# A Mamba kernel with experts: the skip term moves from TensorE to VectorE, the product with silu(z) from VectorE to GpSimd

## Chip, cores, metric

The kernel runs on one core of a Trainium2 chip. The metric is the device time of one execution in microseconds (us), lower being better. Several executions are timed and their median is taken. One further execution is recorded by the hardware profiler.

## What is computed

The input x has 4 sequences of 1024 tokens and 256 channels. It is normalised per token, and two branches use the result. One is eight Mamba layers in a row; the other is a top-1 mixture of eight experts. The output is x + s * silu(experts). The change touches the Mamba layers alone:

```
for i in range(8):
    x = x + mamba_layer(x, ...)
def mamba_layer(x, Wi, cw, cb, Wx, Wdt, bdt, Alog, Dp, Wo):
    xin, z = split(x @ Wi.T, 2)                    # 512 channels each
    u = silu(causal_conv(xin, cw, cb))             # 4 taps
    dt_raw, B, C = split(u @ Wx.T, [16, 16, 16])
    delta = softplus(dt_raw @ Wdt.T + bdt)
    for t in range(1024):                          # the scan, 16 states for each channel
        h = h * exp(delta[t] * A) + (delta[t] * u[t]) * B[t]
        y[t] = sum over states of h * C[t]
    y = (y + u * Dp) * silu(z)
    return y @ Wo.T
```

## The kernel before

The work of the layers is cut into 64 units: 8 layers, 4 sequences, 2 halves of 512 tokens. Even units are the first half of a sequence (`h == 0`), odd ones the second, whose scans start from the state that the first half left (`carry`). Channels lie on the 128 partitions in `CB` = 4 blocks, tokens along the free dimension.

Inside a unit U there are 64 steps: 16 states n times 4 blocks j, numbered k = 4n + j. Each engine walks through these steps (n, j) in its own program and does, at fixed places, the other work of the unit and the preparation of the next two. The places are tables written out by hand at the head of the file (`GATE_AT`, `CONV_AT`, `SOFT_AT`, `RING_AT` and so on). The engines keep in step by semaphores. For one step k:

- GpSimd multiplies `du` (delta times u) by the row of B into `drive` (L884). There are `DRIVE` = 8 drive tiles, so drive k waits until scan k - 8 is over (L883). SyncE fetches the rows of B (`brep`) ahead of it.
- ScalarE makes the decay, exp(delta * A), into one of two PSUM tiles `ps_d` (L916); the exponential k waits for scan k - 2.
- VectorE runs the recurrence over the 512 tokens (`scan`, L1077), which needs decay and drive.
- When the four blocks of a state are scanned, TensorE transposes the state tokens-first into a ring of two PSUM tiles (L1231), ScalarE multiplies by C as it leaves PSUM (`weigh`, L923), and TensorE transposes it back and adds it up in `ps_y` (L1238), whose banks the diagonal products opened.

At places between these, in the unit's order:

- `skip_y` (L1249, TensorE, at (1, 1) and (1, 3)): four products of `u` with a diagonal 128x128 matrix of D, which start the sum in `ps_y`. The matrices of a layer (256 KB) are loaded by SyncE once a layer (L749, L832 to L835), after the last use of those before.
- `gate` (L1177, VectorE, at (1, 1) and three times at (1, 2)): the previous unit's `ps_y` times `zs`, which is silu(z), into `gated`, the tile `relu` under another name.
- two mark operations (L1088, L1090) and the scan of `alive` (L1101) on VectorE at rows 2 and 3, convolution steps of later units (L1114 for a first tap, L1118 for the others), the final sum of the residual `add_x` (L1183), softplus (L1137 to L1147) and `du` (L1127).
- `halo` (L863, L865, GpSimd, at (3, 2)), which waits for the last convolution step of the next unit, `mask_x` (L855, GpSimd, at (5, 1)), and `keep_carry` (L870, GpSimd, once for each state of a first half).
- at (4, 2), ScalarE's block: exponential 20, a table load, silu of the next unit's convolution (`silu_u`, L951), silu of this unit's z (`silu_z`, L955) and a second table load (L1029).
- `x_proj` (L1297) and `out_proj` (L1318) on TensorE; the latter reads `gated`.

Of the kernel before, what the change touches and what calls it, by code (L numbers as in the profile page):

```python
# [73 lines left out]
DRIVE = 8  # L74
# [15 lines left out]
HALO_AT, XM_AT = (3, 2), (5, 1)  # L90
CONV_ITEMS = [f"C{j}" for j in PE_CONV]
CV = CB - len(PE_CONV)
# [563 lines left out]
def mamba(nc, w_in, w_x, w_dt, w_out, w_skip, w_conv, a_log, par, xres, ident, alive_dram, bc_dram, rate_dram):  # L656

    with ExitStack() as ctx:
# [10 lines left out]
        skip = sb("skip", [P, CB, P])  # L669
# [10 lines left out]
        u = sb("u", [P, CB, T])  # L680
# [23 lines left out]
        skip_in, skip_used, conv_w_in = sem("skip_in"), sem("skip_used"), sem("conv_w_in")  # L704
# [27 lines left out]
        def _(sp):  # L732
# [15 lines left out]
            def load_skip(layer):  # L748
                sp.dma_start(skip[:], w_skip[:, layer * CB:(layer + 1) * CB, :]).then_inc(skip_in, 16)  # L749

# [39 lines left out]
            load_skip(0)  # L790
# [11 lines left out]
            for U in range(UNITS):  # L802
                kind = "first" if U == 0 else "last" if U == UNITS - 1 else "near" if U == UNITS - 2 else "mid"
                layer = U // UPL
                if U and kind != "last":
                    load_cur(U + 1, (U + 1) // UPL)
                if kind in ("first", "mid"):
                    load_taps(U, kind, U + 2, (U + 2) // UPL)
                for n in range(BREP, 2 * BREP):
                    load_brep(U, n)  # L810
                if kind in ("first", "mid"):
                    store_alive(U, kind, U + 2)
                if U and U % UPL == 0:

                    sp.wait_ge(ring_ready, item_ready(U, kind, "O1"))
                    load_out(layer)
                for n in range(2 * BREP, STATES):
                    load_brep(U, n)
                if kind != "last":
                    store_bc(U, kind, U + 1)  # L820
                if kind != "last":
                    for n in range(BREP):
                        load_brep(U + 1, n)
                if U % UPL == UPL - 2 and layer + 1 < LAYERS:

                    sp.wait_ge(ring_ready, item_ready(U, kind, "DT3"))
                    load_x(layer + 1)
                    sp.wait_ge(ring_ready, item_ready(U, kind, "Z3"))
                    load_inz(layer + 1)
                    sp.wait_ge(ring_ready, item_ready(U, kind, CONV_ITEMS[-1]))  # L830
                    load_conv(layer + 1)
                if U % UPL == UPL - 1 and layer + 1 < LAYERS:  # L832

                    sp.wait_ge(skip_used, U + 1)
                    load_skip(layer + 1)  # L835
                if U % UPL == UPL - 3 and layer + 1 < LAYERS:

                    sp.wait_ge(ring_ready, item_ready(U, kind, "X3"))
                    load_inx(layer + 1)
# [4 lines left out]
        def _(pool):  # L844
# [57 lines left out]
            units(pool, unit)  # L902

        @block.scalar
        def _(act):
# [40 lines left out]
            def silu_u(U, kind, F):  # L946
                act.wait_ge(conv_done, CV * F + CV)
                act.wait_ge(ring_act, item_read(U, kind, CONV_ITEMS[-1]))
                if not is_first(F):
                    act.wait_ge(skip_used, F)  # L950
                nc.scalar.activation(u[:], xc[:], ACT.Silu).then_inc(u_set, 1)  # L951
# [65 lines left out]
            def unit(U, h, it, kind):  # L1017
                for n in range(STATES):
                    for t in range(TC):
                        k = CB * n + t + 2  # L1020
                        if k < TILES:
                            exponent(U, h, k)
                        elif kind != "last":
                            exponent(U + 1, 1 - h, k - TILES)
                        if (n, t) == SILU_AT:
                            if kind != "last":
                                silu_u(U, kind, U + 1)
# [17 lines left out]
            for n in range(STATES):  # L1045
                for t in range(TC):
                    if (n, t) == SILU_AT:
                        silu_u(0, "pre1", 0)
# [3 lines left out]
            exponent(0, 0, 0)  # L1052
            exponent(0, 0, 1)
# [5 lines left out]
        def _(dve):  # L1059
            def scan(U, h, it, kind, n, j):  # L1060
# [3 lines left out]
                if j == 0:  # L1064
# [10 lines left out]
                    if h == 1 and n < 3:  # L1075
# [45 lines left out]
            def make_du(F, hf, p):  # L1121
# [5 lines left out]
                nc.vector.tensor_tensor(du[:, pair, :], delta[hf][:, pair, :], u[:, pair, :], ALU.mult).then_inc(du_set, 1)  # L1127
# [57 lines left out]
            def unit(U, h, it, kind):  # L1185
                for n in range(STATES):
                    for j in range(CB):
                        scan(U, h, it, kind, n, j)
                        for i in range(CB):
                            if (n, j) == GATE_AT[i] and kind != "first":  # L1190
                                gate(U - 1, 1 - h, i)
# [19 lines left out]
            for j in range(CB):  # L1211
                gate(UNITS - 1, 1, j)
# [4 lines left out]
        def _(pe):  # L1217
# [74 lines left out]
            def x_proj(U, h, kind, F, it):  # L1292
# [3 lines left out]
                for k in range(CB):  # L1296
                    last = nc.tensor.matmul(out[0:XD, :], w_x_sb[:, k, :], u[:, k, :], start=(k == 0), stop=(k == CB - 1))  # L1297
# [31 lines left out]
            def late(U, h, hf, kind, F, it, n, t):  # L1329
# [4 lines left out]
                if (n, t) == RING_AT["XD"]:  # L1334
                    x_proj(U, h, kind, F, it)
# [8 lines left out]
            def unit(U, h, it, kind):  # L1344
                past = kind_before(U, kind)
                for n in range(STATES):
                    for t in range(TC):
# [7 lines left out]
                        for j in range(CB):  # L1355
                            if (n, t) == SKIPY_AT[j]:
                                skip_y(U, kind, it, j)
# [177 lines left out]
```

## Time and profile before

| | |
|---|---|
| time, median of 3 runs | 7741.25 us (7739.77 to 7742.37) |
| the profiled execution's own time | 7743.71 us |
| its span, first to last instruction | 7742.0 us |
| TensorE busy | 6941.3 us, 39999 matmuls |
| VectorE busy | 6668.0 us |
| ScalarE busy | 6422.9 us |
| GpSimd busy | 5929.2 us |
| mean granted TensorE clock | 0.987 of full speed |

Busy time is the union of an engine's instructions; instructions of one engine overlap a little, so durations in a list can add up to more than the busy time. A row of a list has start, duration, engine, line, operation, the tiles written and read, and in brackets the idle time before it with the instruction that ended it.

### The profile page before, as it was taken

How to read it: one execution, taken by the hardware profiler on the slowest of the kernel's cores; microseconds unless marked ns; L12 is line 12 of the kernel's file. 1: busy time of each engine (PE TensorE's matmuls, PEld its weight loads, DVE VectorE, ACT ScalarE, POOL GpSimd, SP SyncE). 2: the span in 40 equal slices, each digit the busy share in tenths (PEclk: the TensorE clock that was granted, in tenths of full speed). 3: DMA queues.
4: the chain of work that ended last, by engine and by line, in shares of the span. 5: the costliest groups of instructions: out<-in, count | busy, mean ns of one | idle time of the engine just before them, and what ended most of it. 6: DMA issues, size and time to landing. Idle time of an engine off the chain costs nothing. (4 is left out here: it accounts for less than half of the span.)

```text
span 7742.0 us, 143629 instructions
## 1 busy us (share of the span) xinstructions
PE 6941.3 (90%) x39999; PEld 4801.8 (62%) x39999; DVE 6668.0 (86%) x6510; ACT 6422.9 (83%) x10314; POOL 5929.2 (77%) x4917
## 2 busy tenths in 40 slices
PE   6979999999999999999999999999999999999997
PEld 4646666666666666666666666666666666666665
DVE  3259988988998899889889988988998898889888
ACT  1258888888888888888888888888888888888887
POOL 2148887888888888888888887888888788888875
PEclk9989999999999999999999999999999999999998
DMA  4111111111111111111111111111111111111112
GB/s 161 34 42 40 40 39 47 43 39 40 42 45 44 39 39 48 42 40 39 40 46 44 40 38 41 45 42 39 39 48 42 39 40 41 45 43 39 40 39 91
DMA packets 222613, 352.40 MB, mean 46 GB/s; under 512 B 43856, under 2 KB 78448, under 8 KB 221712
## 3 DMA queue, kind: packets, MB, share of 16 engines
q1 hardware_dynamic: 218048, 332.70, 14.6%
q0 software_dynamic: 3792, 10.38, 0.4%
q8 instruction: 365, 5.98, 0.3%
q14 instruction: 408, 3.34, 0.1%
HBM read 325.00 MB, written 17.98 MB: 44 GB/s over the span
## 5 line engine op out<-in xcount | busy, mean ns | idle before, releaser
L884 POOL TENSOR_TENSOR drive<-du,brep 128x512 f32<-128x512 f32 x4096 | 5505.9, 1374 | 708.3 <-DVE du L1127 385.6
L916 ACT ACTIVATE ps_d<-delta,cur 128x512 f32<-128x512 f32 x4096 | 2869.9, 701 | 373.9 <-DVE state L1077 354.8
L923 ACT ACTIVATE prod<-ps_r,cT 128x512 f32<-128x512 f32 x4096 | 2837.1, 693 | 245.4 <-PE ps_r L1231 243.9
L1231 PE MATMUL ps_r<-ident,state 128*128 128x128 f32 x16384 | 2564.0, 280 | 297.1 <-ACT prod L923 158.3
L1077 DVE TENSOR_TENSOR_SCAN state<-ps_d,carry,drive 128x512 f32<-128x512 f32 x2048 | 2517.7, 1266 | 260.6 <-ACT ps_d L916 258.5
L1077 DVE TENSOR_TENSOR_SCAN state<-ps_d,drive 128x512 f32<-128x512 f32 x2048 | 2396.8, 1206 | 245.6 <-ACT ps_d L916 233.0
L1238 PE MATMUL ps_y<-ident,prod 128*128 128x128 f32 x16384 | 2481.9, 276 | 25.9 <-ACT prod L923 25.9
L1238 PEld LDWEIGHTS ps_y<-ident,prod 128*128 128x128 f32 x16384 | 1938.9, 142 | 666.8 <-issue 499.4
L1231 PEld LDWEIGHTS ps_r<-ident,state 128*128 128x128 f32 x16384 | 1851.3, 142 | 729.9 <-ACT prod L923 462.5
L1278 PE MATMUL ps_r<-xm,w_inz_sb 128*128 128x512 f32 x1024 | 507.4, 618 | 81.6 <-ACT prod L923 81.6
L1270 PE MATMUL ps_r<-xm,w_inx_sb 128*128 128x512 f32 x1024 | 509.1, 620 | 21.9 <-ACT prod L923 14.2
L1318 PE MATMUL ps_r<-relu,w_out_sb 128*128 128x512 f32 x1024 | 473.9, 606 | 58.6 <-ACT prod L923 56.0
L1118 DVE SCALAR_TENSOR_TENSOR xc<-xpad,taps,xc 128x512 f32<-128x512 f32 x576 | 506.6, 880 | 2.6
L870 POOL COPY carry<-state 128x4 f32<-128x4 f32 x512 | 227.2, 444 | 222.2 <-DVE state L1077 222.1
L1311 PE MATMUL ps_r<-xdbl,w_dt_sb 16*128 16x512 f32 x512 | 295.0, 656 | 86.7 <-DVE xres L1183 52.1
L1318 PEld LDWEIGHTS ps_r<-relu,w_out_sb 128*128 128x128 f32 x1024 | 184.7, 190 | 272.8 <-issue 217.4
L1278 PEld LDWEIGHTS ps_r<-xm,w_inz_sb 128*128 128x128 f32 x1024 | 173.6, 189 | 260.4 <-ACT prod L923 126.7
L1270 PEld LDWEIGHTS ps_r<-xm,w_inx_sb 128*128 128x128 f32 x1024 | 175.1, 190 | 193.1 <-issue 149.3
L535 ACT ACTIVATE hid<-ps_t,b_sb 128x128 f32<-128x128 f32 x312 | 85.0, 383 | 227.4 <-PE ps_t L496 227.3
L1114 DVE TENSOR_SCALAR xc<-xpad,taps 128x512 f32<-128x512 f32 x192 | 189.2, 985 | 93.2 <-ACT xpad L929 93.2
L463 POOL DMA_INDIRECT ys_dram<-yb,row x39 | 37.5, 962 | 296.9 <-DVE yb L555 296.9
L1297 PE MATMUL ps_r<-u,w_x_sb 128*48 128x512 f32 x512 | 234.1, 601 | 33.3 <-ACT u L951 33.3
(144 smaller groups left out, 4647.3 us busy)
## 6 DMA issues: line engine op xcount, KB each, us to landing
brep<-bc_dram SPq DMA_DIRECT2D x1024, 256.0 KB, 3.2
w_sb<-w SPq DMA_DIRECT2D x8, 1024.0 KB
w_all<-w SPq DMA_DIRECT2D x8, 1024.0 KB, 11.4
xb<-xs_dram SPq DMA_DIRECT2D x39, 128.5 KB, 2.0
w_all<-x SPq DMA_DIRECT2D x4, 1024.0 KB, 9.1
w_inx_sb<-w_in SPq DMA_DIRECT2D x8, 512.0 KB, 4.1
w_inz_sb<-w_in SPq DMA_DIRECT2D x8, 512.0 KB, 4.5
w_out_sb<-w_out SPq DMA_DIRECT2D x8, 512.0 KB, 4.2
```

What stands on the lines that cost most here:

```text
L884: nc.gpsimd.tensor_tensor(drive[:, k % DRIVE, :], du[:, j, :], brep[:, n % BREP, :], ALU.mult).then_inc(drive_set, 1)
L916: nc.scalar.activation(ps_d[:, k % 2, :], delta[h][:, j, :], ACT.Exp, scale=cur[h][:, a:a + 1]).then_inc(decay_set, 1)
L923: nc.scalar.activation(prod[:, t, :], ps_r[:, item_place(U, h, kind, item), :], ACT.Copy, scale=cT[(h + 1) % 2 if item[1] == "prev" else h ...
L1077: nc.vector.tensor_tensor_scan(state[STATE_IN[n]][:, j, :], ps_d[:, k % 2, :], drive[:, k % DRIVE, :], carry[:, n, j:j + 1] if h == 1 else ...
L1118: step = nc.vector.scalar_tensor_tensor(xc[:, j, :], xpad[:, j, tap:tap + T], w, xc[:, j, :], ALU.mult, ALU.add)
L1231: last = nc.tensor.transpose(out[:, j * P:(j + 1) * P], state[STATE_IN[n]][:, j, t * P:(t + 1) * P], ident[:])
L1238: last = nc.tensor.matmul(ps_y[:, j, t * P:(t + 1) * P], prod[:, t, j * P:(j + 1) * P], ident[:], start=False, stop=True, is_transpose=Tru ...
L1270: last = nc.tensor.matmul(out, w_inx_sb[:, k, j * P:(j + 1) * P], xm[h][:, k, :], start=(k == 0), stop=(k == DB - 1))
L1278: last = nc.tensor.matmul(out, w_inz_sb[:, k, j * P:(j + 1) * P], xm[hf][:, k, :], start=(k == 0), stop=(k == DB - 1))
L1297: last = nc.tensor.matmul(out[0:XD, :], w_x_sb[:, k, :], u[:, k, :], start=(k == 0), stop=(k == CB - 1))
L1311: nc.tensor.matmul(out, w_dt_sb[:, j * P:(j + 1) * P], xdbl[0:RANK, :], start=True, stop=True).then_inc(ring_ready, 1)
L1318: last = nc.tensor.matmul(out, w_out_sb[:, j, k * P:(k + 1) * P], gated[:, j, :], start=(j == 0), stop=(j == CB - 1))
```

## The change

The sum in `ps_y` now starts with the first state's transposed-back tile (`start=(item[1] == 0)` in `turn_back`), which waits until the previous unit's `ps_y` has been read. The diagonal products, their matrices and their loads go; `skip` becomes a tile of D itself, 32 columns, loaded once. Where VectorE multiplied by `zs`, it now computes u * D + `ps_y` into `gated`, at the same places. GpSimd multiplies `gated` by `zs` in place, one block at each of the steps (3, 0) to (3, 3), behind that step's drive, and `out_proj` and the copy of the next z wait for that. Since `u` is read later than before, there are two u tiles in turn; to hold them, the drive tiles go from 8 to 4, so drive k waits for scan k - 4. The list of exponentials is written as a table (`DECAYS`) with two empty lists of exceptions, and the condition of one carry wait is put in another form (`last < 0` for `n < 3`).

```
-DRIVE = 8
+DRIVE = 4
+BOOST_AT, REST_AT = [], []
-GATE_AT, SKIPY_AT = [(1, 1), (1, 2), (1, 2), (1, 2)], [(1, 1), (1, 3), (1, 3), (1, 3)]
+GATE_AT, ZED_AT = [(1, 1), (1, 2), (1, 2), (1, 2)], [(3, 0), (3, 1), (3, 2), (3, 3)]
...
-        u = sb("u", [P, CB, T])
+        u = [sb(f"u{h}", [P, CB, T]) for h in range(2)]
...
-                if U % UPL == UPL - 1 and layer + 1 < LAYERS:
-
-                    sp.wait_ge(skip_used, U + 1)
-                    load_skip(layer + 1)
...
+            def gate(U, h, j):
+
+                if j == 0:
+                    pool.wait_ge(z_set, U + 1)
+                wait_counted(gated_done, CB * U + j + 1)
+                nc.gpsimd.tensor_tensor(gated[:, j, :], gated[:, j, :], zs[h][:, j, :], ALU.mult).then_inc(zed, 1)
...
+                        for i in range(CB):
+                            if (n, j) == ZED_AT[i] and kind != "first":
+                                gate(U - 1, 1 - h, i)
...
+            for j in range(CB):
+                gate(UNITS - 1, 1, j)
...
-                    act.wait_ge(gated_done, CB * (F - 1))
+                    act.wait_ge(zed, CB * (F - 1))
...
-            def gate(U, h, j):
+            def add_skip(U, h, it, j):
 
                 if j == 0:
                     dve.wait_ge(back_done, TILES * U + TILES)
-                    dve.wait_ge(z_set, U + 1)
-                nc.vector.tensor_tensor(gated[:, j, :], ps_y[:, j, :], zs[h][:, j, :], ALU.mult).then_inc(gated_done, 1)
+                    dve.wait_ge(skip_in, 16)
+                nc.vector.scalar_tensor_tensor(gated[:, j, :], u[h][:, j, :], skip[:, bass.ds((it // BATCH) * CB + j, 1)], ps_y[:, j, :],
+                                               ALU.mult, ALU.add).then_inc(gated_done, 1)
...
+                if item[1] == 0 and t == 0 and kind != "first":
+                    pe.wait_ge(gated_done, CB * U)
                 for j in range(CB):
                     last = nc.tensor.matmul(ps_y[:, j, t * P:(t + 1) * P], prod[:, t, j * P:(j + 1) * P], ident[:],
-                                            start=False, stop=True, is_transpose=True, skip_group_check=True)
+                                            start=(item[1] == 0), stop=True, is_transpose=True, skip_group_check=True)
...
-            def skip_y(U, kind, it, j):
-
-                if kind != "first":
-                    pe.wait_ge(gated_done, CB * (U - 1) + j + 1)
-                if j == 0:
-                    pe.wait_ge(skip_in, 16 * (it // BATCH) + 16)
-                    pe.wait_ge(u_set, U + 1)
-                last = nc.tensor.matmul(ps_y[:, j, :], skip[:, j, :], u[:, j, :], start=True, stop=True, skip_group_check=True)
-                if j == CB - 1:
-                    last.then_inc(skip_used, 1)
...
-                pe.wait_ge(gated_done, CB * V + CB)
+                pe.wait_ge(zed, CB * V + CB)
```

## Rows read from the trace of the kernel before

**Rows 1.** The page, busy time, share and instructions of each engine.

```profile
PE 6941.3 (90%) x39999; PEld 4801.8 (62%) x39999; DVE 6668.0 (86%) x6510; ACT 6422.9 (83%) x10314; POOL 5929.2 (77%) x4917
```

**Rows 2.** The instructions of L951 and of L1114: duration min/median/max, first and last start.

```profile
L951 ACT ACT_TABLE_LOAD  x64: 1283/1283/1283, 469.2 to 7510.8; - x64
...
L1114 DVE TENSOR_SCALAR xc<-xpad,taps x192: 514/547/2268, 459.1 to 7478.6; 128x512 f32<-128x512 f32 x192
```

**Rows 3.** Timeline of VectorE in an odd unit: start, duration, instructions, idle before.

```profile
3993.80 1.13 DVE L1118 SCALAR_TENSOR_TENSOR xc<-xpad,taps,xc 128x512 f32<-128x512 f32 x1
...
4001.46 2.45 DVE L1077 TENSOR_TENSOR_SCAN state<-ps_d,carry,drive 128x512 f32<-128x512 f32 x2
4003.83 0.66 DVE L1088 TENSOR_SCALAR low<-xres 128x1024 bf16 x1
...
4008.56 0.72 DVE L1118 SCALAR_TENSOR_TENSOR xc<-xpad,taps,xc 128x512 f32<-128x512 f32 x1
...
4011.57 7.13 DVE L1077 TENSOR_TENSOR_SCAN state<-ps_d,carry,drive 128x512 f32<-128x512 f32 x6
...
4025.95 1.28 DVE L1077 TENSOR_TENSOR_SCAN state<-ps_d,carry,drive 128x512 f32<-128x512 f32 x1 [3.56 <-ACT ps_d L916]
...
4095.26 2.35 DVE L1127 TENSOR_TENSOR du<-delta,u 128x1024 f32<-128x1024 f32 x2
```

**Rows 4.** Timeline of ScalarE in the same unit.

```profile
4012.86 0.69 ACT L916 ACTIVATE ps_d<-delta,cur 128x512 f32<-128x512 f32 x1 [1.05 <-DVE state L1077]
...
4017.61 0.69 ACT L916 ACTIVATE ps_d<-delta,cur 128x512 f32<-128x512 f32 x1
...
4034.10 0.69 ACT L916 ACTIVATE ps_d<-delta,cur 128x512 f32<-128x512 f32 x1 [2.17 <-DVE state L1077]
```

**Rows 5.** Timeline of GpSimd in the same unit.

```profile
3993.12 9.54 POOL L884 TENSOR_TENSOR drive<-du,brep 128x512 f32<-128x512 f32 x7
4009.61 0.20 POOL L863 COPY xpad<-xpad 128x12 f32<-128x12 f32 x1 [6.95 <-DVE xc L1118]
4009.76 8.66 POOL L884 TENSOR_TENSOR drive<-du,brep 128x512 f32<-128x512 f32 x7
...
4096.64 7.39 POOL L884 TENSOR_TENSOR drive<-du,brep 128x512 f32<-128x512 f32 x5 [6.72 <-DVE du L1127]
```

**Rows 6.** Groups by line and shape: count, busy us, mean ns, idle before.

```profile
L1118 DVE SCALAR_TENSOR_TENSOR xc<-xpad,taps,xc 128x512 f32<-128x512 f32 x576 | 506.6, 880 | 2.6
...
L1249 PE MATMUL ps_y<-u,skip 128*128 128x512 f32 x512 | 241.0, 593 | 0.1
...
L1114 DVE TENSOR_SCALAR xc<-xpad,taps 128x512 f32<-128x512 f32 x192 | 189.2, 985 | 93.2 <-ACT xpad L929 93.2
...
L1177 DVE TENSOR_TENSOR relu<-ps_y,zs 128x512 f32<-128x512 f32 x256 | 160.9, 667 | 5.1 <-PE ps_y L1238 5.1
```

**Rows 7.** Timeline of TensorE in the odd unit.

```profile
3998.99 1.02 PE L1249 MATMUL ps_y<-u,skip 128*128 128x512 f32 x2
...
4000.73 2.74 PE L1249 MATMUL ps_y<-u,skip 128*128 128x512 f32 x6
...
4016.59 3.70 PE L1318 MATMUL ps_r<-relu,w_out_sb 128*128 128x512 f32 x8 [0.53 <-ACT prod L923]
```

**Rows 8.** Timeline of VectorE: the even unit before, and L1114 in both.

```profile
3882.42 1.08 DVE L1118 SCALAR_TENSOR_TENSOR xc<-xpad,taps,xc 128x512 f32<-128x512 f32 x1
...
3890.16 2.33 DVE L1077 TENSOR_TENSOR_SCAN state<-ps_d,drive 128x512 f32<-128x512 f32 x2
...
3899.86 6.77 DVE L1077 TENSOR_TENSOR_SCAN state<-ps_d,drive 128x512 f32<-128x512 f32 x6
...
3918.43 1.15 DVE L1114 TENSOR_SCALAR xc<-xpad,taps 128x512 f32<-128x512 f32 x1 [1.33 <-ACT xpad L929]
...
4029.98 2.10 DVE L1114 TENSOR_SCALAR xc<-xpad,taps 128x512 f32<-128x512 f32 x1 [1.05 <-ACT xpad L929]
```

**Rows 9.** Timeline of GpSimd: a drive of the even unit.

```profile
3882.90 1.73 POOL L884 TENSOR_TENSOR drive<-du,brep 128x512 f32<-128x512 f32 x1
```

More of the change, by code:

```diff
@@ L90 @@
 HALO_AT, XM_AT = (3, 2), (5, 1)
+LEAD = 2
 CONV_ITEMS = [f"C{j}" for j in PE_CONV]
+DECAYS, at = {}, LEAD
+for n, j in [(n, j) for n in range(STATES) for j in range(CB)]:
+    count = 1 + BOOST_AT.count((n, j)) - REST_AT.count((n, j))
+    DECAYS[n, j] = list(range(at, at + count))
+    at += count
 CV = CB - len(PE_CONV)
@@ L668, in mamba @@
         taps = [sb(f"taps{h}", [P, NTAP]) for h in range(2)]
-        skip = sb("skip", [P, CB, P])
+        skip = sb("skip", [P, LAYERS * CB])
         minus_ones = sb("minus_ones", [P, P], BF16)
@@ L789, in _ @@
             load_inz(0)
-            load_skip(0)
+            sp.dma_start(skip[:], w_skip).then_inc(skip_in, 16)
             load_out(0)
@@ L944, in copy_c, with silu_u @@
                                      bias=taps[hf][:, COL_CB + j:COL_CB + j + 1]).then_inc(ring_act, 1)
-            def silu_u(U, kind, F):
+            def silu_u(U, kind, F, hf):
                 act.wait_ge(conv_done, CV * F + CV)
                 act.wait_ge(ring_act, item_read(U, kind, CONV_ITEMS[-1]))
-                if not is_first(F):
-                    act.wait_ge(skip_used, F)
-                nc.scalar.activation(u[:], xc[:], ACT.Silu).then_inc(u_set, 1)
+                if kind == "mid" or kind == "near":
+                    act.wait_ge(gated_done, CB * (F - 1))
+                nc.scalar.activation(u[hf][:], xc[:], ACT.Silu).then_inc(u_set, 1)
             def silu_z(U, h, kind):
@@ L1019, in unit @@
                     for t in range(TC):
[L1020 to L1024, printed above, removed]
+                        for k in DECAYS[n, t]:
+                            if k < TILES:
+                                exponent(U, h, k)
+                            elif kind != "last":
+                                exponent(U + 1, 1 - h, k - TILES)
                         if (n, t) == SILU_AT:
                             if kind != "last":
-                                silu_u(U, kind, U + 1)
+                                silu_u(U, kind, U + 1, 1 - h)
                             silu_z(U, h, kind)
@@ L1047, in _ @@
                     if (n, t) == SILU_AT:
-                        silu_u(0, "pre1", 0)
+                        silu_u(0, "pre1", 0, 0)
                         nc.scalar.preload_act_table_set(TABLE)
@@ L1051, in _ @@
                     early(0, 0, "pre1", 1, n, t)
-            exponent(0, 0, 0)
-            exponent(0, 0, 1)
+            for k in range(LEAD):
+                exponent(0, 0, k)
             units(act, unit)
@@ L1074, in scan @@
                         dve.wait_ge(carried, STATES * it + last + 1)
-                    if h == 1 and n < 3:
+                    if h == 1 and last < 0:
                         dve.wait_ge(carried, STATES * it + last + STATES + 1)
@@ L1126, in make_du @@
                     dve.wait_ge(drive_set, TILES * F - 2 + 2 * p)
-                nc.vector.tensor_tensor(du[:, pair, :], delta[hf][:, pair, :], u[:, pair, :], ALU.mult).then_inc(du_set, 1)
+                nc.vector.tensor_tensor(du[:, pair, :], delta[hf][:, pair, :], u[hf][:, pair, :], ALU.mult).then_inc(du_set, 1)
             def softplus(F, hf, p, part):
@@ L1190, in unit @@
                             if (n, j) == GATE_AT[i] and kind != "first":
-                                gate(U - 1, 1 - h, i)
+                                add_skip(U - 1, 1 - h, it - 1 + h, i)
                         if (n, j) in ADD_AT and kind != "first":
@@ L1211, in _ @@
             for j in range(CB):
-                gate(UNITS - 1, 1, j)
+                add_skip(UNITS - 1, 1, ITERS - 1, j)
             for k in range(DB):
@@ L1290, in conv_pe, with x_proj @@
                 last.then_inc(ring_ready, 1)
-            def x_proj(U, h, kind, F, it):
+            def x_proj(U, h, hf, kind, F, it):
                 out = place(U, h, kind, "XD")
@@ L1296, in x_proj @@
                 for k in range(CB):
-                    last = nc.tensor.matmul(out[0:XD, :], w_x_sb[:, k, :], u[:, k, :], start=(k == 0), stop=(k == CB - 1))
+                    last = nc.tensor.matmul(out[0:XD, :], w_x_sb[:, k, :], u[hf][:, k, :], start=(k == 0), stop=(k == CB - 1))
                 last.then_inc(ring_ready, 1)
@@ L1334, in late @@
                 if (n, t) == RING_AT["XD"]:
-                    x_proj(U, h, kind, F, it)
+                    x_proj(U, h, hf, kind, F, it)
                 if (n, t) == RING_AT["BC"]:
@@ L1354, in unit @@
                             turn_state(U, h, kind, ("S", n - 1, t), U, n - 1, t)
-                        for j in range(CB):
-                            if (n, t) == SKIPY_AT[j]:
-                                skip_y(U, kind, it, j)
                         for k in range(DB):
@@ L1512 @@
         "w_out": blocks(a["attn_W_out"].transpose(0, 2, 1), CB),
-        "w_skip": diagonals(a["attn_D_par"]),
+        "w_skip": by_layer("D_par"),
         "w_conv": diagonals(taps),
```

4 lines of the change are left out of this document (1 added, 3 removed).

## The prediction

> **What bounds the kernel now.** The page's busy shares come first: TensorE 90%, VectorE 86%, ScalarE 83%, GpSimd 77% [rows 1]. No engine is alone at its limit, so a share can't say what one saved or added operation is worth; the place in the period of one unit must. 64 units of 512 tokens pass, one every 111.8 us on average: the 64 starts of silu(u) run from 469.2 to 7510.8 [rows 2]. Odd units (second half of a sequence) and even ones differ a little, so I read one of each.
>
> The timeline of VectorE in an odd unit [rows 3] shows a stretch with no idle mark, from the convolution step at 3993.80 (just before scan 5) to scan 19 at 4018.7. In it lie the four gates, two mark operations, two more convolution steps and the scan of alive. ScalarE comes next [rows 4]. The exponential at 4017.61 is that of scan 20; it waits for the end of scan 18 (the fifth of the six scans that begin at 4011.57 and take 7.13: it ends at 4017.5). Right behind it stand a table load, silu(u), silu(z) and a second load, and only then the exponential of scan 21; VectorE idled 3.56 us for it and began the scan at 4025.95 [rows 3]. So the unit goes: VectorE solid up to scan 18, then ScalarE's block, then the scans again. Whatever delays scan 18 delays the rest of the unit, and what TensorE does meanwhile is inside that cover unless it is very late.
>
> GpSimd [rows 5] runs up to eight tiles ahead. It finishes drive 14 early, waits 6.95 us for the last convolution step (halo, L863), then makes seven drives in 8.66 us, 1.24 each. It is ahead of VectorE throughout.
>
> **The change, part by part** (us per unit; "slower" positive).
>
> TensorE's diagonal products. Two passes of four products start 0.43 apart: 8 x 0.43 = 3.4 us per unit, and the group sums to 241 us over the run [rows 6, 7]. They stand at 3998.99 and 4000.73 to 4003.5, wholly inside VectorE's solid stretch, and ScalarE waited again for VectorE at 4012.86 (1.05 us), after they were done [rows 4]. I take 0. If that cover were gone it would be worth up to -3.4.
>
> The add of the skip term. VectorE's gate is a two-input operation with one input in PSUM, 667 ns [rows 6]. The new one adds a pointer scalar whose address is computed per unit. The nearest row is the convolution step, the same instruction with two SBUF inputs: 0.72 alone (4008.56) and 0.88 as a mean [rows 3, 6]. So 0 to 0.21 each; I take 0.06, as one input stays in PSUM: 4 x 0.06 = +0.25, range 0 to 0.8. All of it is before scan 18, so it counts in full.
>
> Products with silu(z) on GpSimd. Four 128x512 operations like a drive, 1.24 apart: 4 x 1.24 = 5.0 us of GpSimd. On average there is room (77% busy), but they are put between drives 12 and 16, and with four drive tiles drive k can't start before scan k-4 has ended. Odd unit: scan 8 is the first of the two scans from 4001.46 that take 2.45 together, and ends at 4002.7 [rows 3]. From there GpSimd must make drives 12 to 16 and the four products, nine operations: 9 x 1.24 = 11.15, plus the halo copy 0.15: 4014.0. Scan 16 started at 4011.57 + 2 x 1.175 = 4013.9. Late by 0.1 with GpSimd undisturbed. Even unit: scan 8 ends at 3891.35, 11.15 plus a carry copy (0.15) and the memset of the halo (0.05) gives 3902.7; scan 16 started at 3899.86 + 2 x 1.115 = 3902.1 [rows 8]. Late by 0.6.
>
> But GpSimd won't be undisturbed. Before, it stood idle from 4002.6 to 4009.6 [rows 5], while VectorE did two marks and a convolution step (0.66, 0.66, 0.72). The pairs [rows 5, 9] show that these engines hinder each other. A drive that meets a convolution step takes 1.73 in place of 1.24, and that step took 1.08 and 1.13 in place of 0.72 [rows 3, 8, 9]; the first convolution step (L1114) took 1.15 and 2.10 when drives ran beside it [rows 8]; its shortest is 0.51, its median 0.55 [rows 2]. With three such meetings at 0.45 each, GpSimd is later by 1.35; if VectorE gives way instead, it loses 0.3 to 1.5 a meeting, which is the same delay in another row. Scan 16 is then late by 1.45 (odd) and 1.95 (even); up to scan 18 GpSimd's pitch (1.24) against the scans' (1.175 and 1.115), and in even units another carry copy, add 0.1 and 0.4. Mean: (1.55 + 2.35)/2 = +2.0. Bounds: (0.2 + 1.0)/2 = 0.6 without any hindrance, 3.3 if each meeting costs 0.9.
>
> The Trainium skill, SBUF — State Buffer, section "SBUF: two separate sides", says that VectorE and GpSimd take a shared port pair as an exclusive lock for a whole instruction, and the loser blocks fully. By that, all 2.04 us of the three VectorE operations would be added to GpSimd's run in place of 1.35, and this term would be 2.7, which makes 7873 in all. The lengthened rows agree with its kind; no run here yet shows its size in this stretch.
>
> Fewer drive tiles, elsewhere. Later in the unit GpSimd has room again: xm and the drives after it have 6.5 us, the scans stand still during ScalarE's block. There the shorter lead helps. L1114 at 4029.98 (2.10 long) ran while GpSimd made drives 29 and 30, tiles that with four buffers can't be begun before scans 25 and 26. GpSimd will have done drive 26 by about 1.3 after scan 22 and then be silent, so L1114 takes some 0.6 (odd, gain 1.5) and 0.55 in place of 1.15 (even, gain 0.6). ScalarE waited 2.17 for the scan behind it [rows 4], so the gain is on the path: -1.05. Two more convolution steps in even units lie as well, worth some -0.3 to -0.4 in the mean. Sum -1.4, bounds 0 and -2.9: the whole excess of both convolution lines over their shortest times, 506.6 - 576 x 0.72 = 92 and 189.2 - 192 x 0.514 = 91 [rows 2, 6], over 63 units; 0.72 is the lone step of rows 3.
>
> The end of a unit. GpSimd used to be silent for 6.72 us until du was made [rows 5], and the last delta operations and both du (2.35 together) ran undisturbed [rows 3]. Now drives 62 and 63 fall there. Four operations can each be caught, by up to a drive's length; most start together with a scan's end, ahead of GpSimd. +0.5, bounds 0 and 1.4.
>
> At nothing: the second u buffer (its wait is for gates long past), the wait of the projections for the products (done near 4013.5; O0 started at 4016.59 [rows 7]), the turn-back's wait for the add of the skip term (it comes before scan 7, and the turn-back is TensorE's next row of work), the loads of skip that go from SyncE's queue (seven of 256 KB, behind which brep loads stood; each was hidden), the rewritten carry wait, and the list of exponentials, which stays in order. If the products were late for O0 they would cost what they are late beyond 3 us. The tail: the last four products run after the last adds, 4 x 1.24 against 0.6 a gate: +3 once.
>
> **Sum.** 0.25 + 2.0 - 1.4 + 0.5 = +1.35 per unit, x 63 = +85, and 3 at the end: 88. The profiled execution spans 7742.0 and lasted 7743.7, 2.5 above the median of three (7741.25), which is a third of a thousandth, so: 7741 + 88 = about 7829, or +1.1%.
>
> **Rivals.**
> 1. Faster, by relief of the contention. One mechanism: with a lead of four tiles GpSimd moves in step with the scans, and VectorE's two-input operations start ahead of it all through the unit. For it: the 183 us of excess; against: the crowded stretch between drives 12 and 16, of which the pairs above tell. It decides once that relief exceeds the lateness at scan 16. Relief 2.4 against 0.6 + 0.25 + 0.1: -1.45 x 63 = -91, so 7653 with the tail. Chance 0.14.
> 2. A cancelling of the two: lateness 1.3, relief 1.4, the rest 0.1. 7741 to 7752; chance 0.1.
> 3. TensorE's relief pays after all, -3.4 x 63 = -215 and the other terms as in the sum: 7614. Against it is VectorE's solid stretch. Chance 0.05.
> 4. The lock at full size, or VectorE losing at each meeting (2.10 in place of 0.52 shows that this happens): lateness 3.3, relief 1.0, du 1.2, adds 0.4: +3.9 x 63 = +246, 7990 at the worst, 7870 to 7920 more likely. Chance 0.18. For it: the rows of contended pairs; against: most pairs that start together cost one engine only. The rule cited above is the mild form of it.
>
> My forecast has 0.53. Within 0.2% (15 us, about what a measurement can tell from no change): the second rival's part, 0.1; faster 0.19; slower 0.71. Range 7700 to 7920; the forecast's own is 7765 to 7880.
>
> **What the next profile would show.** VectorE's solid stretch should break before scan 16, with GpSimd (L884) as the releaser, or else the marks (L1088, L1090) should be longer than 0.66. ScalarE's block should start 1.5 to 3 us later after scan 0. L1114 should fall from 985 ns to about 600. TensorE's share falls by 3 points. The gate line should show 0.67 to 0.75. I am wrong if GpSimd is never a releaser of a scan and the marks keep their 0.66, or if the removal of the diagonal products alone shortens the unit.

## The result

The changed kernel takes 7968.2 us (median of 4 runs, 7967.9 to 7970.5) where the kernel before took 7741.8: a ratio of 1.0293, 95% interval 1.0276 to 1.0311, 226 us slower. I had forecast 7829, with a range up to 7920. The direction was right, the size less than half of what came, and the time lies outside the range.

The page of the changed kernel, busy time and share, against [rows 1]:

```profile
PE 6841.5 (86%) x39487; PEld 4705.4 (59%) x39487; DVE 6728.4 (84%) x6510; ACT 6442.7 (81%) x10314; POOL 6442.9 (81%) x5173
```

TensorE lost 100 us of busy time, not the 241 of its diagonal products: `out_proj` alone got 66 us slower, and most of the rest is that instructions overlap less. VectorE gained 60, GpSimd 514. The groups by line show where; two groups of the kernel before come first, and [rows 6] have those that answer to L1130, L1126 and L1189 (there L1118, L1114 and L1177):

```profile
L1318 PE MATMUL ps_r<-relu,w_out_sb 128*128 128x512 f32 x1024 | 473.9, 606 | 58.6 <-ACT prod L923 56.0 <-DVE relu L1177 2.7
L1127 DVE TENSOR_TENSOR du<-delta,u 128x1024 f32<-128x1024 f32 x128 | 150.4, 1215 | 0.0
```

```profile
L1322 PE MATMUL ps_r<-relu,w_out_sb 128*128 128x512 f32 x1024 | 539.7, 676 | 139.2 <-ACT prod L935 133.1
...
L1130 DVE SCALAR_TENSOR_TENSOR xc<-xpad,taps,xc 128x512 f32<-128x512 f32 x576 | 482.4, 838 | 2.6
...
L1126 DVE TENSOR_SCALAR xc<-xpad,taps 128x512 f32<-128x512 f32 x192 | 107.1, 558 | 92.8 <-ACT xpad L941 92.8
L1189 DVE SCALAR_TENSOR_TENSOR relu<-u,skip,ps_y 128x512 f32<-128x512 f32 x256 | 176.0, 726 | 5.1 <-PE ps_y L1253 5.1
...
L1139 DVE TENSOR_TENSOR du<-delta,u 128x1024 f32<-128x1024 f32 x128 | 218.3, 1744 | 0.0
```

The adds of the skip term (L1189) take 0.73 where the gates took 0.67. L1126, the first convolution step, fell from 985 ns to 558: the relief that was forecast came. But `out_proj` (L1322) went from 606 to 676 ns a matmul, and du (L1139) from 1.21 to 1.74 us.

The timeline of VectorE in an even unit of the changed kernel, which begins at 3979.51; then GpSimd's in the same stretch:

```profile
3995.30 0.87 DVE L1100 TENSOR_SCALAR low<-xres 128x1024 bf16 x1
...
3997.22 0.66 DVE L1102 TENSOR_SCALAR low<-xres 128x1024 bf16 x1
...
4000.05 0.86 DVE L1130 SCALAR_TENSOR_TENSOR xc<-xpad,taps,xc 128x512 f32<-128x512 f32 x1
...
4004.65 1.22 DVE L1089 TENSOR_TENSOR_SCAN state<-ps_d,drive 128x512 f32<-128x512 f32 x1 [0.37 <-POOL drive L891]
4007.28 4.86 DVE L1089 TENSOR_TENSOR_SCAN state<-ps_d,drive 128x512 f32<-128x512 f32 x4 [1.41 <-POOL drive L891]
4015.64 0.69 DVE L1196 TENSOR_TENSOR xres<-xres,ps_r 128x512 f32 x1 [3.50 <-PE ps_r L1322]
...
4022.54 1.22 DVE L1089 TENSOR_TENSOR_SCAN state<-ps_d,drive 128x512 f32<-128x512 f32 x1 [2.04 <-ACT ps_d L928]
```

```profile
3995.58 1.72 POOL L877 TENSOR_TENSOR relu<-relu,zs 128x512 f32<-128x512 f32 x1
3997.26 1.75 POOL L891 TENSOR_TENSOR drive<-du,brep 128x512 f32<-128x512 f32 x1
3998.95 0.19 POOL L870 COPY carry<-state 128x4 f32<-128x4 f32 x1
3999.10 1.27 POOL L877 TENSOR_TENSOR relu<-relu,zs 128x512 f32<-128x512 f32 x1
4000.33 1.72 POOL L891 TENSOR_TENSOR drive<-du,brep 128x512 f32<-128x512 f32 x1
```

The solid stretch of VectorE breaks at scans 15 and 16, released by GpSimd's drives, and in GpSimd's own rows the marks and the convolution step have each lengthened an operation from 1.27 to 1.72 or 1.75: three meetings, as counted in the forecast. What was not in it stands one row later: VectorE waits 3.50 us for O0, the first eight matmuls of `out_proj`. O0 of an even unit of the kernel before, then TensorE's timeline in the changed kernel:

```profile
3905.06 3.67 PE L1318 MATMUL ps_r<-relu,w_out_sb 128*128 128x512 f32 x8 [0.78 <-ACT prod L923]
```

```profile
4007.26 0.66 PE L1244 MATMUL ps_r<-ident,state 128*128 128x128 f32 x4 [0.17 <-ACT prod L935]
4010.13 5.29 PE L1322 MATMUL ps_r<-relu,w_out_sb 128*128 128x512 f32 x8 [2.22 <-ACT prod L935]
```

The windows ahead of O0 and over it, first of the kernel before, then of the changed one (busy us and instructions of TensorE, its weight loads, VectorE, ScalarE and GpSimd; granted TensorE clock, DMA share, GB/s):

```profile
3900.00:3905.00 5.00, 3.71 (x28) 3.00 (x28) 5.00 (x5) 4.08 (x8) 5.00 (x6) 1.00 0.23 53
3905.00:3908.80 3.80, 3.74 (x11) 1.80 (x12) 1.63 (x2) 3.77 (x5) 3.80 (x4) 1.00 0.29 69
```

```profile
4003.00:4010.10 7.10, 3.71 (x28) 3.00 (x28) 5.25 (x6) 4.53 (x8) 7.10 (x9) 0.99 0.14 37
4010.10:4015.40 5.30, 5.27 (x10) 2.37 (x11) 2.03 (x2) 5.27 (x6) 5.30 (x5) 0.69 0.19 49
```

The same 28 matmuls that took TensorE 3.71 of 5.00 us before are spread over 7.10 us by the late scans, and then the granted clock of the next 5.3 us was 0.69, a mixture of the 2.4 and the 1.2 GHz level. The eight matmuls of O0 took 5.29 us, against 3.67. This is the rule in even units and not in odd ones: O0 took 5.16 us or more in all of the 29 even units from 4 to 60 and in 7 of the 30 odd ones from 3 to 61, and 3.67 to 3.70 in the same units before.

To see how much each place costs, I took from the traces the start of scan k after the unit's scan 0, averaged over 29 even and 29 odd units (3 to 60), and subtracted that of the kernel before (us, even / odd; k = 64 is the next unit's scan 0). Each column includes what lies to its left. The experiments, which follow below, stand in the same table.

| kernel | 12 | 18 | 22 | 31 | 58 | 60 | 64 |
|---|---|---|---|---|---|---|---|
| changed | 0.28/0.40 | 2.56/2.16 | 3.91/2.51 | 3.49/0.33 | 3.08/0.33 | 5.11/1.83 | 5.10/1.84 |
| 4 drive tiles alone | 0.20/0.26 | 0.19/0.26 | 0.19/0.26 | -0.24/-1.93 | -0.64/-1.92 | 1.38/-0.42 | 1.41/-0.41 |
| products of 8 columns | 0.51/0.58 | 0.65/0.65 | 0.65/0.65 | 0.22/-1.53 | -0.18/-1.53 | 1.84/-0.04 | 1.84/-0.02 |
| products early | 0.87/0.60 | 1.86/1.52 | 1.86/1.52 | 1.43/-0.66 | 1.02/-0.67 | 3.05/0.83 | 3.05/0.85 |
| du late | 0.39/0.61 | 2.66/2.37 | 3.84/2.34 | 3.42/0.16 | 3.01/0.16 | 2.49/-0.80 | 5.92/2.66 |
| transposes twice | 0.40/0.58 | 2.69/2.35 | 2.42/2.33 | 2.00/0.14 | 1.59/0.14 | 3.62/1.64 | 3.61/1.65 |
| no diagonals | -0.02/-0.01 | -0.04/0.07 | -0.04/0.06 | -0.05/-0.29 | -0.12/-0.29 | -0.12/-0.29 | -0.12/-0.25 |
| 4 tiles, du spread | 0.01/0.16 | 0.00/0.16 | -0.01/0.16 | -0.43/-2.02 | 1.00/-0.54 | -0.27/-1.95 | 0.80/-0.81 |
| products in row 2, du spread | 1.44/1.14 | 2.43/2.06 | 2.42/2.06 | 1.98/-0.14 | 3.39/1.31 | 2.13/-0.10 | 3.19/1.04 |
| lead of 4 at 60 to 63 | -0.07/0.00 | -0.06/0.00 | -0.06/0.00 | -0.08/-0.19 | -0.10/-0.21 | 1.42/1.07 | 1.41/2.13 |
| lead of 4 at 20 to 31 | 0.02/0.00 | 0.02/-0.01 | 0.02/0.00 | -0.41/-2.19 | 0.77/0.02 | 0.77/0.01 | 0.77/0.05 |
| lead of 4 at 20 to 39 | -0.05/0.00 | -0.04/-0.01 | -0.04/0.00 | -0.48/-2.19 | -0.59/-0.62 | 0.31/-0.48 | 0.30/0.14 |
| lead of 4 at 24 to 28 | 0.00/0.00 | 0.00/-0.01 | 0.01/0.00 | -0.42/-2.18 | -0.35/-0.34 | -0.35/-0.34 | -0.35/-0.35 |

In the changed kernel a unit is 3.47 us longer in the mean, and 63 of them make 219 of the 226 us. Three places pay: up to scan 18 (2.36), steps 18 to 22 of even units (1.35 there), and the du stretch between scans 58 and 60 (2.03 and 1.50).

### The profile page after: what moved, and what is told of

Its sections match the earlier page's. It is cut to its first block and busy times, and to the rows that moved or that the text cites. A ratio compares the mean times of both kernels' runs of the same rounds, so it can differ in the third digit from the quotient of the medians.

```text
span 7968.7 us, 143200 instructions
## 1 busy us (share of the span) xinstructions
PE 6841.5 (86%) x39487; PEld 4705.4 (59%) x39487; DVE 6728.4 (84%) x6510; ACT 6442.7 (81%) x10314; POOL 6442.9 (81%) x5173
## 5 line engine op out<-in xcount | busy, mean ns | idle before, releaser
L891 POOL TENSOR_TENSOR drive<-du,brep 128x512 f32<-128x512 f32 x4096 | 5741.2, 1422 | 1070.7 <-DVE state L1089 946.4
L1244 PEld LDWEIGHTS ps_r<-ident,state 128*128 128x128 f32 x16384 | 1822.6, 141 | 1076.4 <-ACT prod L935 782.9
L1322 PE MATMUL ps_r<-relu,w_out_sb 128*128 128x512 f32 x1024 | 539.7, 676 | 139.2 <-ACT prod L935 133.1
L1130 DVE SCALAR_TENSOR_TENSOR xc<-xpad,taps,xc 128x512 f32<-128x512 f32 x576 | 482.4, 838 | 2.6
L1322 PEld LDWEIGHTS ps_r<-relu,w_out_sb 128*128 128x128 f32 x1024 | 208.1, 213 | 395.9 <-issue 360.7
L877 POOL TENSOR_TENSOR relu<-relu,zs 128x512 f32<-128x512 f32 x256 | 352.6, 1378 | 8.2 <-issue 8.2
L1196 DVE TENSOR_TENSOR xres<-xres,ps_r 128x512 f32 (+1 forms) x128 | 88.1, 688 | 208.3 <-PE ps_r L1322 208.3
```

The source lines that it names most:

```text
L877: nc.gpsimd.tensor_tensor(gated[:, j, :], gated[:, j, :], zs[h][:, j, :], ALU.mult).then_inc(zed, 1)
L891: nc.gpsimd.tensor_tensor(drive[:, k % DRIVE, :], du[:, j, :], brep[:, n % BREP, :], ALU.mult).then_inc(drive_set, 1)
L1130: step = nc.vector.scalar_tensor_tensor(xc[:, j, :], xpad[:, j, tap:tap + T], w, xc[:, j, :], ALU.mult, ALU.add)
L1244: last = nc.tensor.transpose(out[:, j * P:(j + 1) * P], state[STATE_IN[n]][:, j, t * P:(t + 1) * P], ident[:])
L1322: last = nc.tensor.matmul(out, w_out_sb[:, j, k * P:(k + 1) * P], gated[:, j, :], start=(j == 0), stop=(j == CB - 1))
```

## The experiments

Ratios are against the kernel before on the same chip, with their 95% interval. The chips differ a little: the kernel before had a median of 7739.2 to 7744.8 us beside the experiments, so a difference of two experiments' times can be off by up to 6 us.

**Four drive tiles alone.**

```
-DRIVE = 8
+DRIVE = 4
```

> The kernel before with 4 drive tiles in place of 8 and nothing else. Theory A (the loss of the change is made in three places: GpSimd's crowded run between drives 12 and 16, TensorE's halved clock behind it, and drives 62 and 63 that now lie in front of du): only the third place is left, about +1.1 us per unit, against a gain of 1.5 in odd and 0.6 in even units from L1114; together 7740 to 7790 us. Theory B (the shorter lead itself costs, all over the unit): most of the 226 us, so above 7880.

7779.0 us, ratio 1.0052 (1.0035 to 1.0068), inside theory A's range: the shorter lead costs almost nothing up to scan 22, gains up to scan 31 (0.43 and 2.19) and loses 2.02 and 1.50 between scans 58 and 60. Both sizes were underestimated, a loss of 1.76 per unit in the mean for the 1.1 expected and a gain of 1.3 by scan 31 for 1.05, and the total is right since they offset each other. Of the 226 us the shorter lead explains about 38. The du stretch of an odd unit, VectorE and then GpSimd:

```profile
4106.20 1.62 DVE L1144 TENSOR_TENSOR low<-low,delta 128x1024 f32<-128x1024 f32 x1
4107.73 1.27 DVE L1077 TENSOR_TENSOR_SCAN state<-ps_d,carry,drive 128x512 f32<-128x512 f32 x1
4108.93 1.19 DVE L1147 TENSOR_TENSOR delta<-low,relu 128x1024 f32<-128x1024 f32 x1
4110.05 3.42 DVE L1127 TENSOR_TENSOR du<-delta,u 128x1024 f32<-128x1024 f32 x2
```

```profile
4104.22 7.03 POOL L884 TENSOR_TENSOR drive<-du,brep 128x512 f32<-128x512 f32 x4
4114.74 2.68 POOL L884 TENSOR_TENSOR drive<-du,brep 128x512 f32<-128x512 f32 x2 [3.49 <-DVE state L1077]
```

The two du took 2.35 before [rows 3] and 3.42 here. The last of the four drives (number 63) ends at 4111.25; it was free to start when scan 59 was over, had to let L1147 end, and then, by these rows, went ahead of the first du. L1144 took 1.62 in place of 1.20, since drive 61 was already running when it began. By the traces' means L1144 costs 0.83 in even and 0.42 in odd units, the two du 1.07 and 1.08: nearly the whole of the 2.02 and 1.50. In the code the second du also waits for drive 63, since it overwrites what that reads.

**Products of 8 columns.** GpSimd multiplies 8 of the 512 columns by silu(z); the others are left unmultiplied, which changes what is computed.

```
-nc.gpsimd.tensor_tensor(gated[:, j, :], gated[:, j, :], zs[h][:, j, :], ALU.mult)
+nc.gpsimd.tensor_tensor(gated[:, j, 0:8], gated[:, j, 0:8], zs[h][:, j, 0:8], ALU.mult)
```

> The changed kernel, but GpSimd multiplies only 8 of the 512 columns of each block by silu(z); the other columns are left unmultiplied, so the output is not the reference's. Theory A: the run of GpSimd between drives 12 and 16 loses its four times 1.24 us, scan 18 starts at most 0.4 later than in the kernel before, TensorE has no pause and keeps its clock; 7750 to 7800 us. Theory B (the lead): still above 7880. Theory C (the add of the skip term with its computed address costs more than the 0.25 us per unit of the sum): above 7850 too, with the lengthened operations in the profile.

7806.0 us, ratio 1.0087 (1.0071 to 1.0104), 6 us above theory A's range, with scan 18 later than the 0.4 that it allowed. Without the length of the products 162 us of the 226 are gone, scan 18 is 0.65 late in place of 2.36, and O0 takes 3.70 in every unit: the clock's part of the loss goes with the late scans. The rest, 27 us above 4 tiles alone, bounds what the adds of the skip term and the four small operations cost, less whatever TensorE's relief gives.

**Products early.**

```
-ZED_AT = [(3, 0), (3, 1), (3, 2), (3, 3)]
+ZED_AT = [(2, 1), (2, 2), (2, 2), (2, 3)]
```

> The changed kernel with the four products of GpSimd at steps (2,1), (2,2), (2,2), (2,3), where its trace shows GpSimd idle while VectorE adds the skip terms, in place of (3,0) to (3,3). Theory A: the same 5 us of GpSimd's work cost nothing there, scan 18 is late by 0.3 to 0.8, TensorE's clock stays at 2.4 GHz before O0; 7750 to 7820 us. Rival (GpSimd's work delays the scans wherever it stands, through the shared port): 7900 or more.

7873.5 us, ratio 1.0171 (1.0154 to 1.0188): 95 us better than the changed kernel and 50 to 120 worse than I expected, between the ranges of theory A and of the rival. The products cost something there too: the run is 67 us above the one with 8 columns. Scan 13 waited behind a convolution step that had itself to wait for GpSimd (1.62 in place of 0.72):

```profile
4070.62 2.68 DVE L1089 TENSOR_TENSOR_SCAN state<-ps_d,carry,drive 128x512 f32<-128x512 f32 x2
4073.22 1.62 DVE L1130 SCALAR_TENSOR_TENSOR xc<-xpad,taps,xc 128x512 f32<-128x512 f32 x1
4074.76 1.27 DVE L1089 TENSOR_TENSOR_SCAN state<-ps_d,carry,drive 128x512 f32<-128x512 f32 x1
```

What it saves is more than the scans' lateness: in even units scans 18 and 22 are late by the same 1.86, so O0 no longer adds anything.

**Du late.**

```
-DU_AT = [(14, 3), (14, 3)]
+DU_AT = [(15, 0), (15, 1)]
```

> The changed kernel with the two du operations at steps (15,0) and (15,1) in place of both at (14,3). Theory A: drives 62 and 63 no longer stand in front of the second du, VectorE loses less there: 0.6 to 1.2 us per unit, 7890 to 7930 us. Rival (the first drives of the next unit come too late now, as they wait for du): equal to the changed kernel or slower, with GpSimd as the releaser of scans 0 to 3.

8016.4 us, ratio 1.0355 (1.0338 to 1.0373), 48 us slower than the changed kernel. That is the rival's outcome, but not its mechanism: no scan from 0 to 3 of the next unit waits for GpSimd. Scan 60 starts 2.6 us earlier than in the changed kernel, as the two du now stand behind it, and scan 62 is 0.8 later: in the unit that I looked at, the second du takes 1.41 in place of 1.21 and the convolution step behind it 1.50 in place of 0.52, beside drives 64 and 65. The meeting was moved, not avoided.

**No diagonals.** The kernel before without the four diagonal products; u * D is missing in what is computed.

```
-                last = nc.tensor.matmul(ps_y[:, j, :], skip[:, j, :], u[:, j, :], start=True, stop=True, skip_group_check=True)
                 if j == CB - 1:
-                    last.then_inc(skip_used, 1)
+                    pe.sem_inc(skip_used, 1)
...
-                                            start=False, stop=True, is_transpose=True, skip_group_check=True)
+                                            start=(item[1] == 0), stop=True, is_transpose=True, skip_group_check=True)
```

> The kernel before without the four diagonal products of a unit: the sum in ps_y starts with the first transposed-back tile, the term u * D is left out of the output, all else stays (8 drive tiles, gates on VectorE, loads of skip). Theory A (TensorE's 3.4 us per unit lie in the cover of VectorE's solid stretch): within 10 us of 7740; the start of scan 18 after scan 0 moves by less than 0.1 us. Rival (TensorE's share of 90% was a bound): down to 7530. Second rival (the idle time lowers TensorE's clock later in the unit): 10 to 60 us slower, with more stretches at half the granted clock than the 24 of before.

7728.8 us, ratio 0.9977 (0.9966 to 0.9987). Scan 18 didn't move (-0.04, 0.07), as theory A had it, but the time lies just outside its 10 us: 16 us are gained, mostly in odd units behind scan 22, of the 215 that TensorE's 3.4 us per unit would have been. Where exactly they come from is open. O0 keeps its 3.67 to 3.70 and there are 24 stretches at half the granted clock, as many as before, so taking the products away doesn't by itself lower the clock at O0.

**Transposes twice.** To keep TensorE busy while the scans are late.

```
+TWICE_AT = [(2, 1), (2, 2), (2, 3), (3, 0), (3, 1)]
...
-                for j in range(CB):
-                    last = nc.tensor.transpose(out[:, j * P:(j + 1) * P], state[STATE_IN[n]][:, j, t * P:(t + 1) * P], ident[:])
+                for r in range(2 if (n, t) in TWICE_AT else 1):
+                    for j in range(CB):
+                        last = nc.tensor.transpose(out[:, j * P:(j + 1) * P], state[STATE_IN[n]][:, j, t * P:(t + 1) * P], ident[:])
```

> The changed kernel with the transposes of five state tiles (state 2 from its second token block on, and two of state 3) made twice over the same place, so that TensorE is busier by 0.44 us each in the stretch in which it now waits for the late scans. Theory A (O0 takes 5.29 us in place of 3.67 in even units since TensorE's clock fell to half, and scans 20 and 22 are late for that): O0 is back near 3.7, scan 22 of even units is 1.5 earlier, 7890 to 7930 us. Rival (what is late there is GpSimd's product or ScalarE's order, and the clock only goes with it): 7968 or, with the added work on the path, up to 8000.

7919.6 us, ratio 1.0222 (1.0205 to 1.0239), inside theory A's range: more work on TensorE and 49 us less time. Its windows and its O0 in an even unit that begins at 3955.46:

```profile
3979.00:3986.00 7.00, 5.35 (x46) 4.77 (x44) 5.13 (x6) 4.60 (x8) 7.00 (x9) 1.00 0.10 38
3986.00:3991.40 5.40, 5.00 (x17) 2.54 (x18) 3.49 (x4) 5.37 (x6) 5.40 (x5) 1.00 0.15 52
```

```profile
3986.09 3.70 PE L1324 MATMUL ps_r<-relu,w_out_sb 128*128 128x512 f32 x8 [1.73 <-ACT prod L936]
```

Busy for 5.35 of 7.00 us, TensorE keeps the full clock and O0 takes 3.70 again, in 63 of the 64 units. Scan 22 of even units is late by 2.42 in place of 3.91, while scan 18 is as late as before. Even units are 1.49 shorter and odd ones 0.19, together 52 us for 31 pairs, against the measured 49 (52 if each run is taken against the kernel before on its own chip). So this part of the loss is the clock, not GpSimd's product, and it is a consequence of the late scans.

**Four tiles, du spread.**

```
-SOFT_AT = [(7, 3), (8, 3), (9, 3), (10, 2), (10, 3), (11, 3), (14, 2), (14, 3)]
+SOFT_AT = [(7, 3), (8, 3), (9, 3), (10, 2), (10, 3), (11, 3), (14, 1), (14, 2)]
-DU_AT = [(14, 3), (14, 3)]
+DU_AT = [(14, 3), (15, 0)]
```

> The kernel before with 4 drive tiles, the last two softplus operations at (14,1) and (14,2) in place of (14,2) and (14,3), and the two du at (14,3) and (15,0). Theory A (of what 4 tiles alone cost, 1.5 to 2.0 us per unit come from the first du waiting behind drive 63, and the rest of the unit gains 0.6 to 1.9): the first du no longer meets drive 63, 7660 to 7720 us, faster than the kernel before. Rival (the crowding only moves): equal to the 7779 of the run with 4 tiles alone.

7744.2 us, ratio 0.9998 (0.9989 to 1.0008): 35 us better than 4 tiles alone and equal to the kernel before, not the 20 to 80 faster that I expected. The two du are no longer lengthened, which saves 1.0 to 1.1 us per unit, but scan 60 now waits 0.8 us until its state tile is free, which the two du had covered.

**Products in row 2, du spread.** The changed kernel with the placing above and

```
+ZED_AT = [(2, 0), (2, 1), (2, 2), (2, 3)]
```

> The changed kernel with GpSimd's four products at (2,0) to (2,3) and the same placing of softplus and du as in the run above. Theory A: against the run with the products at (2,1) to (2,3) (7873) one product fewer stands before drive 13, 0.5 to 1 us per unit, and du gives back 1 to 1.8: 7730 to 7790 us. Rival (GpSimd is short of time wherever the products stand): 7850 or more.

7884.1 us, ratio 1.0176 (1.0159 to 1.0193). The rival was right. From scan 31 to the unit's end the new placing of du gives back some 0.4 us per unit (1.21 and 1.18 lost there, 1.62 and 1.51 with the products early), but one product earlier doesn't help: scan 8 is already 1.0 late (the convolution step before it took 1.41 in odd and 1.68 in even units), scan 18 2.43 and 2.06 in place of 1.86 and 1.52. I tried three placings of the products, and none brought the design under 7873.

**A lead of four at some steps only.** These keep 8 tiles and change one wait of GpSimd in the kernel before; the range stood at `k >= 60`, `20 <= k < 32`, `20 <= k < 40` and `24 <= k < 29`.

```
-pool.wait_ge(scanned, TILES * U + k + 1 - DRIVE)
+pool.wait_ge(scanned, TILES * U + k + 1 - (4 if k >= 60 else DRIVE))
```

> The kernel before with its 8 drive tiles, but drives 60 to 63 of a unit wait for the scan four steps back. Theory A (the cost of 4 tiles is made at du, by drives 62 and 63 that fall among the last softplus operations and du): +1.5 to +2.0 us per unit, 7835 to 7870 us. Rival (the loss of 4 tiles at du is one of the whole lead, not of these drives): within 20 us of 7742.

7854.8 us, ratio 1.0142 (1.0127 to 1.0158). Four drives held back at the end of a unit cost 110 us, and the rival is refuted. Between scans 58 and 60 it is 1.52 and 1.28, of the 2.02 and 1.50 with 4 tiles at all steps; in odd units another 1.06 comes behind, since L1114 at step 61 takes 1.58 in place of 0.52.

> The kernel before with its 8 drive tiles, but drives 20 to 31 of a unit wait for the scan four steps back in place of eight; the other drives run ahead as before. Theory A (what 4 tiles gain is the first convolution steps behind ScalarE's block that no longer stand behind two drives, and what they lose is made at du): the gain without the loss, -0.4 us in even and -1.9 in odd units by step 31, as in the run with 4 tiles alone, about 7660 to 7690 us. Rival (the gain of that stretch is given back at the next wait, or the caught-up drives disturb VectorE later by as much): 7720 to 7745.

7765.6 us, ratio 1.0026 (1.0017 to 1.0035). The gain comes to the hundredth as with 4 tiles alone (-0.41 and -2.19 at scan 31) and is given back before scan 39, where GpSimd catches up: L1137, a softplus operation at step 31, takes 1.62 and 1.70 in place of 0.75 and 0.67. The rival had the mechanism; the time is 20 us above its range as well.

> The same for drives 20 to 39. Theory A: as above, and L1114 at step 38 of even units gains another 0.6; 7640 to 7680 us, if GpSimd still gets ahead of VectorE before du. Rival (GpSimd can't get ahead any more in the 20 drives that are left, and meets the last softplus operations): between the run above and 7780.

7757.5 us, ratio 1.0018 (1.0008 to 1.0027). Neither range was hit: 78 us above theory A, 8 below the rival's. It is the same give-back, later: even units still have -0.59 at scan 58 and lose 0.90 by scan 60, at du.

> The kernel before with its 8 drive tiles; only drives 24 to 28 of a unit wait for the scan four steps back. Theory A (the relief of L1114 at step 22 is real and the runs with longer windows gave it back because GpSimd caught up while VectorE did the first softplus operations): GpSimd now catches up in steps 25 to 31, where VectorE has pauses of about 1 us; -0.4 us in even and about -1.2 in odd units remain, 7680 to 7710 us, faster than both kernels. Rival (catching up costs VectorE as much wherever it is done): 7735 to 7765.

7723.8 us, ratio 0.9978 (0.9969 to 0.9987), 18 us faster than the kernel before and the fastest kernel here with the whole computation. It lies between the two ranges, 14 us above theory A's: -0.35 in both kinds of unit, since odd ones give back 1.8 of their 2.18 between scans 31 and 39 (L1137 at step 31 takes 1.76 in place of 0.67). The step at stake, with the two drives gone from beside it (2.10 before, [rows 8]):

```profile
4020.01 0.59 DVE L1114 TENSOR_SCALAR xc<-xpad,taps 128x512 f32<-128x512 f32 x1 [1.05 <-ACT xpad L929]
```

## Why the prediction was wrong

Step by step, forecast against measured, us per unit (mean of even and odd):

- Diagonal products at nothing: measured -0.19 (no diagonals), 12 to 16 us in all. Nearly right: the cover holds up to scan 22, but the forecast had named any shortening by the removal alone as a sign of being wrong, and the ratio's interval excludes 1.
- The add of the skip term +0.25: 726 against 667 ns on the lines, 0.06 x 4 = 0.24. Right; the computed address added nothing that the lines show.
- The products of GpSimd, scan 18 late by 2.0, with the adds 2.25: measured 2.56 and 2.16, mean 2.36. Right in the mean, by the mechanism that was named: nine operations between scan 8's end and drive 16, three of them lengthened by 0.45. Even units were forecast at 2.60, odd ones at 1.80. The split is less exact than the sum: with products of 8 columns 0.65 of the lateness stays, so their length is worth 1.7 and not 2.0, and 0.2 is the shorter lead before scan 12, to which the forecast gave nothing. The Trainium skill, SBUF — State Buffer, section "Who interferes with whom", says that a VectorE instruction with two SBUF inputs, or in a mode that uses both ports, contends with a GpSimd instruction that reads SBUF, while one with at most one SBUF input outside those modes doesn't. The trace agrees: L1189, whose second tensor is in PSUM, took 0.71 to 0.75 in all its 256 instructions, many of them beside running drives.
- Fewer tiles elsewhere -1.4: measured in 4 tiles alone from scan 18 to 58 as -0.83 and -2.18, mean -1.5. Right in the mean, and partly by luck: the terms of the forecast gave even units about 1.3 and odd ones 1.5. L1114 at step 22 shrank as forecast, by 1.49 in odd and 0.60 in even units.
- The end of a unit +0.5, bound 1.4: measured 2.03 and 1.50, mean 1.77 in the changed kernel, and the same in 4 tiles alone. **This step failed.** I took it that most operations of VectorE which start with a scan's end go ahead of GpSimd. That holds for L1147, but L1144 finds a drive already running (+0.84 and +0.42), and drive 63 gets in between L1147 and the first du (+1.08). I also overlooked in the code that the second du must wait for drive 63 in any case. The run with only drives 60 to 63 held back shows that these drives cause 1.40 of the 1.77; the rest goes with the whole lead of four.
- "At nothing" for the wait of the projections, and "what TensorE does meanwhile is inside that cover": **this step failed too**. O0 didn't wait for the products, as forecast, but TensorE, idle beside the late scans, lost its clock, and O0 took 1.6 us longer: +1.35 in even and +0.35 in odd units by scan 22. The forecast listed no term for the clock, though its own late scans were going to leave TensorE idle just ahead of O0. The experiment that only adds transposes gives it 49 us.

The sum of the forecast was 1.35 per unit and 3.47 came. Of the difference of 2.12, du is 1.27; the clock is (1.49 + 0.19)/2 = 0.84; the other terms, +0.1 up to scan 18 and -0.1 for the tiles elsewhere, cancel. The range ended too low, at 7920, since the du term's bound was too low and no term stood for the clock; the rival that gave a larger loss had the right side, but for a reason that didn't occur (VectorE losing at every meeting between drives 12 and 16).

Settled by experiments: the cost of the products' length, of drives 60 to 63, of the clock, and that TensorE's relief was worth 16 us at most in the kernel before. Only argued from rows: that it is drive 63, and not 62, which the first du waits for. Not tried: the changed kernel with eight drive tiles, for which there is no room beside two u tiles.

## What to carry to other kernels

When work goes from the fullest engine to another, look first for the stretch where it stands: here TensorE's 90% was worth 0.2%, and 5 us per unit on an engine that was idle for 23% of the time cost 162 us, because they stood where that engine had a deadline. A buffer's depth is not only protection against waiting: it also sets which operations of the other engine the producer runs beside, and the same convolution step took 2.10 or 0.59 us by that. Relief in one place can be lost at the next: of three kernels that held the drives back only where this helps, one kept a gain. And an engine whose clock depends on its activity can punish a wait a second time, in the work that follows it.

## What the runs showed of the hardware

- A VectorE operation can lose to two GpSimd operations in a row (L1114: 2.10 us where 0.51 is its shortest) and gets its time back when these are moved away (0.59).
- Doubling 20 transposes a unit, 2.2 us more work for TensorE, made the kernel 49 us faster, as the granted clock stayed at 1.00 where it had been 0.69. Nothing but transposes was added.
- TensorE's granted clock fell more often in the changed kernel: 52 stretches at half the full rate, 181 us together, against 24 and 109 us before, counted in the clock records between 520 and 7660 us. The count alone says little: products of 8 columns had 54 stretches (188 us) and transposes twice 46 (157 us), yet O0 took 3.70 in all 64 units of the one and 63 of the other, and 4 tiles with du spread had 2 (7 us) and the time of the kernel before. What matters is whether a stretch falls on work that the scans wait for.
